# New orders of the same steps in the instruction tables of the steady chunk of a fused attention and expert layer

## What is computed

```python
def attention(q, k, v, Wq, bq, Wk, bk, Wv, bv, Wo, bo):      # 16 heads of 32
    qh, kh, vh = heads(q @ Wq + bq), heads(k @ Wk + bk), heads(v @ Wv + bv)
    attn = softmax(einsum('bhqd,bhkd->bhqk', qh, kh) / sqrt(32))
    return concat(einsum('bhqk,bhkd->bhqd', attn, vh)) @ Wo + bo

def experts(x, gate_w, expert_w):                           # 8 experts
    onehot = one_hot(argmax(x @ gate_w.T))
    return x + einsum('bsef,bse->bsf', einsum('bsh,efh->bsef', x, expert_w), onehot)

x = x + attention(layernorm(x), ctx, ctx, ...)
out = x + experts(layernorm(x), gate_w, expert_w)
```

## Time and profile before

| what | us |
|---|---|
| median of three runs | 953.04 (950.65 to 953.06) |
| the profiled execution | 953.55 |
| its span, first to last instruction | 951.7 |
| mean granted clock of TensorE in it | 0.974 of full speed |

### The profile page before, as it was taken

How to read it: one execution, slowest core, us unless ns; L and a number is a source line. 1 busy time by engine, 2 the same in 40 slices (tenths; PEclk the granted TensorE clock), 3 DMA queues, 4 the chain that set the end, 5 groups by cost and what they waited for, 6 DMA issues and landing times. The chain is left out here.

```text
span 951.7 us, 25248 instructions
## 1 busy us (share of the span) xinstructions
PE 902.5 (95%) x8840; PEld 542.2 (57%) x8841; DVE 775.3 (81%) x1794; ACT 557.5 (59%) x928; POOL 523.8 (55%) x576
## 2 busy tenths in 40 slices
PE   5999999999999999999999999998887999999995
PEld 3457566565665655656566565665653555555552
DVE  8998889999899998989999899987884555556652
ACT  4686867768677686876868768665751221122220
POOL 2426463555636556365564655535533777777774
PEclk8998999999999999999999999998797999999998
DMA  9323242434424335243342533228344556555550
GB/s 312 110 57 94 65 146 60 130 95 121 146 54 139 102 100 138 70 140 72 132 146 58 142 94 90 80 54 282 133 156 135 157 172 173 165 166 169 176 170 15
DMA packets 81941, 119.30 MB, mean 125 GB/s; under 512 B 20465, under 2 KB 45797, under 8 KB 81839
## 3 DMA queue, kind: packets, MB, share of 16 engines
q1 hardware_dynamic: 69359, 83.74, 32.3%
q0 software_dynamic: 11408, 34.17, 9.5%
q10 hardware_dynamic: 1072, 0.02, 0.1%
HBM read 55.24 MB, written 38.13 MB: 98 GB/s over the span
## 5 line engine op out<-in xcount | busy, mean ns | idle before, releaser
L529 POOL TENSOR_TENSOR p_lo<-pf,p_hi 77x512 f16<-77x512 f32 x128 | 147.2, 1155 | 203.1 <-ACT p_hi L1156 203.1
L1155 ACT ACTIVATE pf<-scoresT,exp_scale 77x512 f32<-77x512 f32 x256 | 175.1, 684 | 72.5 <-PE scoresT L882 62.8
L1654 PE MATMUL mo<-e_w,x2T_hi 128*128 x576 | 184.1, 381 | 0.7 <-DVE x2T_lo L1691 0.7
L1156 ACT ACTIVATE p_hi<-scoresT,exp_scale 77x512 f16<-77x512 f32 x256 | 175.4, 685 | 0.0
L1674 ACT ACTIVATE x2T_hi<-mt 128x512 f16<-128x512 f32 x72 | 43.0, 597 | 179.7 <-PE mt L1643 179.7
L1701 DVE SCALAR_TENSOR_TENSOR res<-mo,inv,row 128x512 f32<-128x512 f32 x72 | 54.1, 751 | 90.7 <-PE mo L1654 90.7
L529 DVE TENSOR_TENSOR p_lo<-pf,p_hi 77x512 f16<-77x512 f32 x128 | 106.4, 848 | 12.2 <-ACT p_hi L1156 12.1
L1243 DVE TENSOR_REDUCE negmax<-work 128x4 f32<-128x308 f32 x256 | 112.5, 467 | 0.3 <-PE work L934 0.3
L1654 PE MATMUL mo<-e_w,x2T_lo 128*128 x288 | 109.8, 381 | 0.0
L1625 POOL DMA_INDIRECT out<-res,row x72 | 71.5, 994 | 64.6 <-DVE xn L1686 56.3
L854 PE MATMUL work<-wo_hi,cT_hi 128*128 128x512 f16 x256 | 97.3, 380 | 0.4
(11 more groups left out here) (262 smaller groups left out, 2160.9 us busy)
## 6 DMA issues: line engine op xcount, KB each, us to landing
row<-rows_by_expert SPq DMA_DIRECT2D x72, 257.5 KB, 2.9
q_st<-q_hi SPq DMA_DIRECT2D x256, 64.0 KB, 2.0
xt<-in_x SPq DMA_DIRECT2D x15, 1024.0 KB, 7.3
q_st<-q_lo SPq DMA_DIRECT2D x128, 64.0 KB, 2.0
ebuf<-in_L_ffn_expert_w SPq DMA_DIRECT2D x14, 512.0 KB, 8.8
er<-in_L_ffn_expert_w SPq DMA_DIRECT2D x7, 1024.0 KB, 14.8
rows_by_expert<-zrow SPq DMA_DIRECT2D x8, 257.5 KB, 2.7
out<-res,row POOLq DMA_INDIRECT x72, 2.8
```

What stands on the lines that cost most here:

```text
L529: return tt.tensor_tensor(pp[1][0:LK, g % 2, j, :], pf[:, j, :], pp[0][0:LK, g % 2, j, :], ALU.subtract)
L1155: nc.scalar.activation(pf[:, j, :], sbank[n % SB][0:LK, :], ACT.Exp, scale=exp_scale[0:LK, :])
L1156: nc.scalar.activation(pp[0][0:LK, g % 2, j, :], sbank[n % SB][0:LK, :], ACT.Exp, scale=exp_scale[0:LK, :]).then_inc(sem("exp_done"), 1)
L1654: ins = nc.tensor.matmul(obank2[u % 2][:, :], x2T[ia][:, u % 2, k, :], w, start=k == 0 and n == 0, stop=k == KT - 1 and n == 2)
```

## The change

STEPS, VECTOR and SCALAR get new orders. GPSIMD keeps its words, so its order stays; SyncE reads STEPS too, but only for the order of its Q steps, which also stays. The same steps are in each table, once each. No step is added or taken away, and no semaphore, tile or size changes; all lines behind the tables move down by one.

```diff
 STEPS = order("""
-    T0 T1 NM C0 T2 C1 T3 O0 C2 S00 S01 Q0 S02 S03 O1 S10 M00 C3 S11 M01 Q1 S12 PV0 S13 M02 GC M03 M10 S20 S21 M11 M12
-    O2 M13 S22 S23 Q2 R S30 S31 PV1 M20 Q3 S32 M21 S33 M22 PV2 M23 O3 M30 GX PV3 M31 M32 M33
+    T0 C0 NM T1 C1 T2 T3 O0 C2 S00 S01 Q0 S02 C3 S03 O1 S10 M00 M01 S11 Q1 S12 M02 S13 PV0 GC M03 S20 M10 M11 M12 S21
+    Q2 S22 M13 O2 R S23 M20 S30 PV1 M21 Q3 M22 S31 M23 S32 O3 S33 PV2 M30 M31 M32 GX PV3 M33
 """)
 VECTOR = order("""
-    T0 T1 NM C0 T2 C1 K T3 O0 B0 P00 P01 C2 Q0 O1 M00 B1 L0 C3 M01 L1 P10 P11 L2 Q1 M02 GC M03 L3 M10 M11 H P20 LE P21
-    M12 V00 V01 O2 M13 B2 Q2 R V10 V11 M20 SL P30 Q3 V20 M21 M22 M23 V21 P31 O3 M30 B3 GX VE V30 M31 M32 M33 V31
+    T0 C0 NM T1 C1 K T2 T3 O0 C2 B0 P00 P01 Q0 C3 O1 M00 L0 M01 L1 L2 P10 P11 Q1 V00 M02 GC M03 L3 M10 M11 P20 B1 H LE
+    P21 M12 Q2 V01 M13 O2 R M20 B2 V10 M21 V11 P30 SL Q3 M22 P31 M23 O3 V20 B3 V21 VE M30 M31 V30 V31 M32 GX M33
 """)
 SCALAR = order("""
-    T0 T1 C0 T2 C1 T3 S00 S01 C2 Q0 S02 S03 C3 S10 S11 Q1 S12 S13 EX0 S20 S21 S22 S23 Q2 X0 S30 S31 Q3 S32 X1 X2 S33 X3
+    T0 C0 T1 C1 T2 T3 C2 S00 S01 Q0 C3 S02 S03 S10 S11 Q1 S12 S13 S20 S21 Q2 S22 S23 X0 S30 Q3 S31 S32 S33 X1 EX0 X2
+    X3
 """)
```

## The result

| | before | after |
|---|---|---|
| median, us | 952.59 (950.25 to 953.06, 6 runs) | 974.35 (969.23 to 982.8, 6 runs) |
| ratio, 95% interval | | 1.0243 (1.0213 to 1.0273) |
| profiled execution, us | 953.55 | 978.27 |
| its span, us | 951.7 | 976.4 |

What follows compares the result with a forecast made beforehand. VectorE's chain from O3 to O0 at each chunk boundary was taken as the bound, with TensorE idle 1.62 us per chunk. 953.55 + 0.8 - 0.5 = 953.8, plus 2.7 for three clock falls, gave 956.5 us; range 950.0 to 961.0.

Steps and rivals of the forecast that it cites:

- parts 1 to 3: Chunk boundary, O3's end to O0: 0.27 us gained, waits of 0.14 and 0.17 added; stall 1.68 against 1.62 per chunk.
- the two waits: VectorE at the boundary: a wait of 0.14 us ahead of V20 and one of 0.17 ahead of T1's drain.
- case C: Boundary: neither predicted VectorE wait shows and the clock stays; 949.5 us, chance 0.16.
- case A: Boundary: the worked-out chain alone, with no clock falls; 953.8 us, chance 0.28.
- part 4: Middle of the chunk: banks are drained in time, ScalarE's moved steps fit its idle time; price 0.
- case B: Boundaries: the chain plus three falls of TensorE's clock at 0.9 us each, +2.7; 956.5 us, chance 0.42.
- part 5: SyncE's queue: later query transfers, nmT landing 2.4 us after issue, hidden in most chunks; price 0, 0.9 at worst.
- case D: nmT lands late or a middle bank isn't drained, without the clock; 959.4 us at 0.4 per chunk, chance 0.14.

Runs made afterwards that it cites:

- c6_wide10: The kernel before with ten dummy matmuls of 512 columns behind M33 in the steady chunks; 983.4 us, ratio 1.0322.
- e2: The changed kernel with VectorE's K moved behind Q0 and GpSimd's key copy moved behind D; 964.24 us, ratio 1.0136.
- c1_head: The kernel before with the new head order alone, and V31 directly behind V30 on VectorE; 955.49 us, ratio 1.003.
- e3: The changed kernel with dummy matmuls of 512 columns, three behind T0 and two behind C0; 972.49 us, ratio 1.0228.
- e5: The changed kernel with the edits of e2 and e3 together; 965.53 us, ratio 1.0124.
- c5_narrow84: The kernel before with 84 dummy matmuls of 33 columns behind M33 in the steady chunks; 979.83 us, ratio 1.028.
- e1: The changed kernel with the steady chunks' nmT transfer issued by ScalarE instead of SyncE; 1015.92 us, ratio 1.0636.
- e7: The changed kernel with the old head order put back on TensorE, VectorE and ScalarE; 979.3 us, ratio 1.0275.
- e8: The changed kernel with e2's moves, and SyncE's loads of x and weights held until nmT has landed; 963.64 us, ratio 1.0115.
- e11: The changed kernel with the edits of e2 and e1, and SyncE's two loads held until nmT has landed; 959.33 us, ratio 1.0088.
- c2: The kernel before with S33 alone moved behind O3 on TensorE; 992.01 us, ratio 1.042.
- e4: The changed kernel with the edits of e1, e2 and e3 together; 1000.57 us, ratio 1.0493.
- e6: The changed kernel with S33 put back ahead of O3 on TensorE, PV2 staying behind O3; 974.23 us, ratio 1.0224.
- b1: The kernel before with e2's two moves (K behind Q0, GpSimd's key copy behind D); 969.17 us, ratio 1.0172.
- c3: The kernel before with 48 dummy matmuls of 33 columns behind M33 in the steady chunks; 955.84 us, ratio 1.0049.
- e10: The changed kernel with e2's moves and two 512-column dummy matmuls per steady chunk, behind GX and M33; 960.82 us, ratio 1.0116.
- e12: The changed kernel with the edits of e10 and e11 together; 956.35 us, ratio 1.0042.

## Why the prediction was wrong

**The chain (parts 1 to 3) held, a little too dear.** O3's end to O0 is 9.00 us in undisturbed chunks, 9.19 was worked out; with 7.51 of TensorE's own work the stall is 1.49, not 1.68. Neither of the two waits showed: VectorE runs from O3's drain to T1's without a gap. One of them was also too large by its own terms: VectorE was said to come to T1 from 6.40, where M33's end had been worked out at 6.48, and from there the wait is 0.09. So on the chain alone, case C was a little nearer than case A.

**The middle (part 4) held on TensorE**: S02 to O3 is 1.41 shorter in all plain chunks, the 1.43 that moved out, and no new stall came. But this part looked at TensorE's banks alone. K and GpSimd's additions are not among them, and they are where the price of 0 failed.

**The step that failed most is one that wasn't there.** The prediction took each VectorE operation at its duration from the trace and never asked whether GpSimd runs beside it. T0 came 1.1 us later against the end of the chunk on VectorE, and with it K against A0: GpSimd's first scatter in chunks 3, 7 and 11 stands at T0 + 2.73 to 2.75 before and at T0 + 1.55 to 1.68 after. Taking K and the key copy out of the way is worth 10.1 us, nearly half of the loss, with the falls and waits that go with them.
The Trainium skill, SBUF — State Buffer, section Who interferes with whom, has the rule: copies and additions of a constant on VectorE that use both port pairs share one with GpSimd, and whoever issues first keeps the other engine out for the whole instruction. The rows agree that one engine is kept out (5.00 us beside A0 to A2, 1.08 beside the key copy); they don't show who came first, since the copy that was held in c6_wide10 starts 0.61 us before the additions.

**The clock (case B) was the right mechanism with the wrong count and, in part, the wrong cause.** Nine boundaries instead of three; the price of one, 0.5 to 1.06 (0.8 on average in e2), was near the 0.9 taken. It was put down to the new stops and to the longer stretch without a wide product. But c1_head has longer stops and no fall; four of the nine falls had begun before T0 and so before the stop behind it; and with the stops filled only the falls behind T0 are gone, those ahead of it are not (e3, e5). Neither did 9 us without wide work bring it (c5_narrow84, with the reservation made there). Shown is only this: with S33 behind O3 the clock fell at 4 to 11 boundaries (after, e1, e2, e3, e5, e7, e8, e11, c2; at one in e4, whose chunks are 40 to 47 us long by the waits for nmT); with S33 ahead (before, e6, b1, c1, c3 to c6) it fell at one boundary at most; and with S33 behind O3 but two wide matmuls ahead of T0 (e10, e12) never. What of the order between O3 and T0 it takes stays open.
The Trainium skill, TensorE: Matmul & The Clock Gate, section A second HAM failure mode, puts such falls down to small stops between groups of matmuls. Here the run with the longest stops has none, so the measurement decides against it as the sole cause; that it has a part in the falls behind T0 agrees with e3 and e5.

**The transfer of nmT (part 5, case D) was priced at 0 and cost some 7 us**, 7.3 by the waits. The stack's end was right (O3's end + 8.5 to 9.2; 8.1 to 9.3 worked out), and so was nmT's drain (7.6 to 8.3 in plain chunks). The term that failed is the landing: 2.4 us is the median of a kernel in which the queue had been empty for 1.1 us. Right behind twelve transfers of 64 KB the median is 4.35 (3.5 over all chunks). The issue at 9.1, with the scores at 12.0, leaves 2.9 us; a wait was to be expected in most undisturbed chunks. A median was also the wrong figure for it: in the kernel before, 5 of 14 landings took over 2.9 us already. What lengthens the landing stays open: not the loads behind it (e8_hold), and not the stack directly ahead alone (3.1 in e6_s33).

**The cases were taken as rivals, and all came at once.** By the runs: K and the key copy 10.1, the clock and nmT 7.9 together (964.24 to 956.35), 4.0 left, against a gain of 0.11 a chunk from the chain. The single shares of the clock and of nmT aren't separated: each acts on the other. A range made of one case at a time ended at 961.

## What to carry to other kernels

When an order changes, lay VectorE and GpSimd side by side, not only each against TensorE: a copy of 0.25 us can take 4 if GpSimd's run of additions starts within 0.4 us of its end, and a distance of 0.7 us is a thin margin. Take the landing time of a transfer from places where the queue ahead of it looks as it will after the change, and hold its spread, not its median, against the time that is left; and sum the risks of one boundary, since a delay of one kind sets off the others. A plain period that is 0.3% shorter is worth little if it uses up all slack at the places where it repeats.

## What the runs showed of the hardware

- A held copy waits for the whole run of GpSimd's additions, not for one: a single 32x308 copy took 4.2 to 4.4 us beside three additions of 1.26 us (e7_head, c5_narrow84), though GpSimd ends an instruction in between.
- Wide dummies ahead of T0 (two) took all falls of the clock away; five behind T0 and C0 left 4 of 10 (e3) and 6 of 7 (e5), all of them starting ahead of T0.
- A transfer of 16 KB landed after 6.4 to 7.4 us where a load of 1 MB had been issued just before it on another queue, and after 2.7 to 3.8 where it was issued first (e1_nmt_act, 7 and 5 chunks).
- 1.3 us more work for an engine that is 95% busy cost 0.43 us a chunk (c3_narrow): it went into the stops. Only beyond these does it cost its full time (0.90 for the next 36 matmuls).
- 28 of the 384 issues of query transfers took 0.95 to 2.2 us instead of 0.6 in the changed kernel, 25 in the kernel before, one to three in each chunk. In the changed kernel, where nothing lies between the stack and nmT, that alone moves nmT's issue by some tenths from one chunk to the next.
